# Cross-attention on one core: row sums on TensorE, late query spreads, and keys in twelve tiles of 121

## The reference

```python
Q = relu(queries @ Wq + bq); K = relu(keys @ Wk + bk); V = relu(values @ Wv + bv)
scores = einsum('hbqd,hbkd->hbqk', Qh, Kh) * scale
key_mask = sign(abs(sum(keys, axis=-1)))        # rows that sum to 0 are masked
scores = where(key_mask == 0, NEG, scores)
attn = softmax(scores, axis=-1)
q_mask = sign(abs(sum(queries, axis=-1)))       # and so are query rows that sum to 0
attn = attn * q_mask
out = einsum('hbqk,hbkd->hbqd', attn, Vh) + queries
```

## Time and profile before

| | us |
|---|---|
| median of three runs | 380.84 (379.0 to 381.56) |
| the profiled execution | 380.48 |
| its span, first to last instruction | 378.7 |
| TensorE matmuls busy | 357.3 (94%) |
| ScalarE busy | 303.9 (80%) |
| VectorE busy | 240.4 (63%) |
| mean granted clock | 0.995 |

### The profile page before, as it was taken

The page is one execution under the profiler, slowest core; times in us unless marked ns, Lnnn a source line. Parts: engine busy times, 40 slices in busy tenths (PEclk is TensorE's granted clock), DMA queues, the critical chain, the costliest instruction groups (busy, mean ns, idle before and its releaser), DMA issues.

```text
span 378.7 us, 16915 instructions
## 1 busy us (share of the span) xinstructions
PE 357.3 (94%) x6712; PEld 252.0 (67%) x6712; DVE 240.4 (63%) x785; ACT 303.9 (80%) x405; POOL 5.7 (2%) x20
## 2 busy tenths in 40 slices
PE   7997898799999999999999999999999999799991
PEld 5655666467676767676776767676776767577660
DVE  5797948267593939576684939485775937475202
ACT  2487477678888888888888888888888888689990
POOL 4010000000000000000000000000000000000000
PEclk9999999999999999999999999999999999999997
DMA  7529904956383745646373846547363837245100
GB/s 222 137 76 326 340 7 88 335 190 209 109 286 86 271 130 185 212 153 191 134 243 85 303 99 221 178 159 227 126 210 103 295 89 263 62 151 175 13 3 8
DMA packets 42852, 63.42 MB, mean 167 GB/s; under 512 B 28426, under 2 KB 32842, under 8 KB 42826
## 3 DMA queue, kind: packets, MB, share of 16 engines
q1 hardware_dynamic: 42106, 62.15, 51.8%
q10 hardware_dynamic: 720, 0.89, 0.7%
HBM read 14.55 MB, written 0.82 MB: 41 GB/s over the span
## 4 chain that ended last, share of the span: by engine, by line
PE 82%; DVE 6%; SPq 3%; DMA 3%; issue 2%; ACT 1%; DVEq 0%; ACTq 0%
PE psum L564 31%; PE psum L549 26%; PE psum L516 12%; PE psum L508 11%; SPq L334 3%; DMA k_parts<-k_low 3%; PE psum L636 1%; DVE v_biased L810 1%; PE psum L647 1%; DVE values L820 1%; DVE selectors L989 1%; ACT probs L477 1%; ACT k_parts L467 1%; DVE q_sum L946 1%; SPq L301 1%
## 5 line engine op out<-in xcount | busy, mean ns | idle before, releaser
L477 ACT ACTIVATE probs<-psum 128x800 f32<-128x800 f32 x384 | 293.5, 840 | 53.3 <-PE psum L549 53.3
L564 PE MATMUL psum<-probs,values 128*32 128x200 f32 x3072 | 153.7, 333 | 0.0
L549 PEld LDWEIGHTS psum<-query_bd,k_parts 64*128 64x128 f32 x1536 | 96.1, 187 | 44.9 <-issue 40.0
L564 PEld LDWEIGHTS psum<-probs,values 128*32 128x32 f32 x3072 | 97.8, 110 | 40.8 <-issue 19.1
L549 PE MATMUL psum<-query_bd,k_parts 64*128 64x200 f32 x1536 | 120.0, 286 | 1.6 <-DMA k_parts<-k_low 1.4
L773 DVE TENSOR_SCALAR_CACHE_REDUCE k_raw<-psum,bk_sb 128x361 f32<-128x361 f32 (+2 forms) x63 | 37.7, 600 | 88.3 <-PE psum L508 88.2
L508 PE MATMUL psum<-keyT,wk_mixed 128*32 128x361 f32 (+2 forms) x504 | 52.4, 491 | 6.2 <-DMA keyT<-in_ctxT 2.2
L516 PE MATMUL psum<-wv_sb,keyT 128*32 128x129 f32 x1536 | 55.1, 277 | 3.3 <-DVE v_biased L810 3.3
L820 DVE TENSOR_SCALAR values<-v_biased,keep 128x128 f32<-128x128 f32 x192 | 43.8, 289 | 6.4
L516 PEld LDWEIGHTS psum<-wv_sb,keyT 128*32 128x32 f32 x1536 | 38.4, 109 | 10.8 <-DVE v_biased L810 4.0
L810 DVE TENSOR_TENSOR v_biased<-psum,bv_sb 128x384 f32<-128x384 f32 x64 | 35.1, 548 | 0.0
(11 more groups left out here) (64 smaller groups left out, 81.7 us busy)
## 6 DMA issues: line engine op xcount, KB each, us to landing
k_parts<-k_high SPq DMA_DIRECT2D x30, 722.0 KB, 5.0
k_parts<-k_low SPq DMA_DIRECT2D x30, 722.0 KB, 5.5
keyT<-in_ctxT SPq DMA_DIRECT2D x15, 722.0 KB, 4.4
query_rep<-k_parts SPq DMA_DIRECT2D x4, 800.0 KB, 8.0
residual<-in_x SPq DMA_DIRECT2D x64, 12.5 KB
out<-residual SPq DMA_DIRECT2D x64, 12.5 KB
x_sb<-in_x SPq DMA_DIRECT2D x1, 800.0 KB
values<-in_xT ACTq DMA_DIRECT2D x1, 600.0 KB, 6.7
```

The costliest lines, as they stand in the source:

```text
L477: nc.scalar.activation(probs[:, u % PROB_SLOTS], scores_ps[:, u % SCORE_SLOTS, :, 0:QCOLS], ACT.Exp, scale=SCALE).then_inc(probs_ready, 1)
L549: mm = nc.tensor.matmul(scores_ps[:, u % SCORE_SLOTS, j, n * TCOLS:(n + 1) * TCOLS], k_parts[rows, parity, t, kt * P:(kt + 1) * P], query_ ...
L564: mm = nc.tensor.matmul(o_spans[c * VCOLS:(c + 1) * VCOLS, half, :, :, 0:SPAN], values[:, parity, kt, half * HALF_PAIRS + c, :], probs[:, ...
```

## The change

1. **Tiles of 121.** Score matmuls, exponentials, value projections and value products use twelve tiles of 121 keys (12 x 121 = 1452) in place of 128. In a value projection the last column group has 25 keys, not 32.
2. **Row sums on TensorE.** `x_sb`, its load and VectorE's sums are gone. TensorE multiplies the transposed queries with a column of ones, 16 matmuls of one column, as the first side work of batch 0; VectorE compares. A matrix made by GpSimd (`row_pick`) then spreads the mask over the partitions by four matmuls in the last cycle of batch 0, in place of the 16 copies.
3. **Queries in two spreads.** The first group (batches 0 to 3) is split and copied at the start as before. The other three groups (1200 columns) are cast and subtracted in `first_batch` between key reads, and their four copies stand in SyncE's queue behind the spread keys of batch 2. Every batch of the loop waits for `late_replicated` before it spreads queries.
4. **Order.** At the start the weights are mixed before the selectors are made, and the bias of the keys is loaded first. The residuals of batches 0 and 1 are loaded earlier. In `first_batch` a value read stands between the two centerings, and the queries are spread before the last value read. The query maximum, the bounds (now one operation) and the head sums move to the end of batch 14.

```diff
+    KTILE = -(-SK // KT)
+    SKT = KT * KTILE
...
-                    for g in range(SPANS):
-                        at = c * VCOLS
-                        sp.dma_start(row_mask[at:at + SPAN, g, :], q_mask[g * SPAN:(g + 1) * SPAN, :]
-                                     ).then_inc(rows_masked, 16)
...
-            for ready, count, source, slots in ((q_high_ready, 1, q_high, (0, 1)), (q_split, 3, q_low, (2, 3))):
+            sp.wait_ge(pads_zeroed, 4)
+            sp.wait_ge(first_evacuated, KCHUNKS)
+            load_residual(0, 0)
+            load_residual(1, 1)
+
+            for ready, count, source, slots in ((q_relued, 2, q_high, (0, 1)), (q_split, 2, q_low, (2, 3))):
...
             sp.wait_ge(scores_ready, UNITS)
             spread_keys(2, 0)
+            for ready, source, slots in ((late_high_ready, late_high, (0, 1)), (late_split, late_low, (2, 3))):
+                sp.wait_ge(ready, 1)
+                for n in slots:
+                    sp.dma_start(query_rep[n:P:SLOTS, :, QB * SQ:].bitcast(F32),
+                                 source[:].rearrange("p g n -> p (g n)").bitcast(F32)).then_inc(late_replicated, 16)
...
+            def sum_queries(index):
+
+                work(index)
+                for b in range(B):
+                    mm = nc.tensor.matmul(work_ps[0:SQ, b:b + 1], xT_sb[:, b * SQ:(b + 1) * SQ], ones[:, 0:1],
+                                          start=True, stop=True)
+                mm.then_inc(work_filled, 1)
+
+            def pick_rows(index):
+
+                work(index)
+                pe.wait_ge(rows_picked, 2)
+                for g in range(SPANS):
+                    mm = nc.tensor.matmul(work_ps[:, g * B:(g + 1) * B], row_pick[:, g, :], q_mask[:],
+                                          start=True, stop=True)
...
-                                              k_parts[rows, parity, t, kt * P:(kt + 1) * P],
+                        mm = nc.tensor.matmul(scores_ps[0:KTILE, u % SCORE_SLOTS, j, n * TCOLS:(n + 1) * TCOLS],
+                                              k_parts[rows, parity, t, kt * KTILE:(kt + 1) * KTILE],
                                               query_bd[rows, parity, t, :], start=True, stop=True)
...
-            FIRST_SIDE_WORK = (((0, NEXT),), ((1, NEXT), (2, NEXT)), ((3, NEXT), VALUES[0]), VALUES[1:2], VALUES[2:3],
-                               (VALUES[3], KEYS[0]), KEYS[1:3], KEYS[3:4])
+            FIRST_SIDE_WORK = (((SUM, NEXT), (0, NEXT)), ((1, NEXT), (2, NEXT)), ((3, NEXT), VALUES[0]), VALUES[1:2],
+                               VALUES[2:3], (VALUES[3], KEYS[0]), KEYS[1:3], (KEYS[3], (ROWS, NEXT)))
...
             def first_batch():
-                read_keys(1, 0, 0)
-                max_queries()
...
+                mask_queries(0)
...
+                read_keys(2, 0, used)
+                high_queries()
+                read_keys(2, 1, used + 1)
+                read_keys(2, 2, used + 2)
+                low_late_queries()
+                read_keys(2, 3, used + 3)
...
+                dve.wait_ge(late_replicated, 16 * SLOTS)
                 spread_queries(b + 1, 1 - parity)
                 finish_keep(b + 1, 1 - parity)
-                bound_scores(b + 1, 1 - parity)
```

More of the change, by code:

```diff
@@ L512, in project_values @@
             def project_values(bank, parity, g, n):
-                at = (g * VGROUP + n) * P
-                for m in range(0, P, VCOLS):
-                    mm = nc.tensor.matmul(bank[m:m + VCOLS, n * VW:(n + 1) * VW],
-                                          keyT[:, parity, at + m:at + m + VCOLS], wv_sb[:], start=True, stop=True)
+                at = (g * VGROUP + n) * KTILE
+                for m in range(0, KTILE, VCOLS):
+                    end = min(m + VCOLS, KTILE)
+                    mm = nc.tensor.matmul(bank[m:end, n * VW:(n + 1) * VW],
+                                          keyT[:, parity, at + m:at + end], wv_sb[:], start=True, stop=True)
                 return mm
@@ L573, in _ @@
             NEXT, AFTER = 1, 2
+            SUM, ROWS = -1, -2
             KEYS = tuple((c, AFTER) for c in range(KPARTS))
@@ L600, in batch @@
                     units = range(cycle * CYCLE, (cycle + 1) * CYCLE)
-                    for step in side[cycle][:-1]:
+                    early = 0 if first and cycle == 0 else max(len(side[cycle]) - 1, 0)
+                    for step in side[cycle][:early]:
                         side_work(step)
@@ L607, in batch @@
                         pe.wait_ge(first_k_spread, KCHUNKS * QUADS)
-                    for step in side[cycle][-1:]:
+                    for step in side[cycle][early:]:
                         side_work(step)
```

240 lines of the change are left out of this document (121 added, 119 removed).

## The result

| | before | changed |
|---|---|---|
| median of the runs made together | 380.63 us | 385.72 us (383.98 to 388.19) |
| ratio | | 1.016, 95% interval 1.011 to 1.021 |
| profiled execution, time and span | 380.48, 378.7 us | 386.32, 384.6 us |
| mean granted clock | 0.995 | 0.971 |

The changed kernel is slower by 5.1 us in the medians and by 5.8 us between the two profiled executions. The forecast was 384.8 us.

What follows compares the result with a forecast made beforehand. TensorE was taken to bound steady batches, ScalarE's exponentials the last twelve cycles, waits the first two batches. 380.5 - 3.3 + 1.9 + 3.2 + 2.2 + 0.3 = 384.8 us, range 379 to 390.

Steps and rivals of the forecast that it cites:

- A: The forecast itself: 384.8 us in total, own range 382.5 to 388, chance 0.48.
- 1. Tiles of 121: -3.3: Score matmuls, batches 2 to 13 and half of 14: shorter key loads save 0.033 us in each of 100 cycles, -3.3 us.
- D: Rival at the score loads: 111 ns is a floor whatever the columns, so tiles give nothing; 388.8 us, chance 0.15.
- E: Rival at the score loads: 121 columns lose a quick form of load that 128 have; 592 us, chance 0.02.
- 2 and 3. Batch 0: +1.9: Batch 0: row sums and row picker add 4.4 us on TensorE, fewer waits and faster scores take off 2.3 and 0.3.
- 4. The late copies: 8.3 us of wait, +3.2: Batch 1: old waits go, but TensorE waits 8.3 us through VectorE for late query copies; 29.1 against 25.9 us.
- 5. The clock: +2.2: Behind batch 1's wait for late copies: TensorE's clock falls to the lower level, costing 2.2 us.
- 6. The start: +0.3: Ahead of batch 0: query weights load later behind bias and first x slice, between -0.4 and +0.7, taken as +0.3 us.
- 7. VectorE's stand: 0: Behind VectorE's loop: its 3.21 us stand without a releaser, of which TensorE lost 2.1, stays as it was.
- Rival F: The wait at VectorE's stand moves with the code, -2.1 us (382.7), or another appears, +2; chance 0.04.

Runs made afterwards that it cites:

- tiles128: The changed kernel with key tiles of 128 columns again, all else of the change kept; 391.39 us, 1.030 of the kernel before.
- before121: The kernel before with only its key tiles changed, twelve of 121 in place of 128; 375.65 us, ratio 0.988.
- late_first: The changed kernel with the four late query copies issued ahead of the spread keys of batch 2; 374.77 us, 0.985 of the kernel before.
- peel: The changed kernel with VectorE's batch 1 written out ahead of its loop, without the wait for late copies there; 372.10 us, 0.977 of the kernel before.
- peel_wait: The changed kernel with VectorE's batch 1 written out ahead of its loop, its wait for late copies kept; 382.69 us, 1.007 of the kernel before.
- before121_peel: The kernel before with tiles of 121 and VectorE's batch 1 written out before its loop, row sums still on VectorE; 374.42 us, ratio 0.985.
- one_sum: The changed kernel with one matmul of ones replacing the row-sum matmuls, so every query row counts as kept; 380.42 us, 1.003 of the kernel before.
- both_start: The changed kernel with late copies first, batch 1 written out without the wait, 32-column row sums, and ScalarE's old load order; 368.14 us, 0.969 of the kernel before.
- wide_sums: The changed kernel with each row-sum matmul moving 32 columns of ones instead of one; 386.69 us, 1.016 of the kernel before.

## Why the prediction was right, and what it left out

The forecast, A, held: 384.8 us against 385.72, with the wait where and how it was put. By its own steps, measured between the two profiled executions:

**1. Tiles of 121: -3.3.** Measured -3.20 over 92 cycles, 0.035 us each instead of 0.033. tiles128 and before121 confirm it from both sides. Rivals D, a floor of 111 ns, and E, a slow load at 121 columns, are out: a load of 121 columns takes 182 ns, and the 100-column loads of the sums go every 89 ns, the interval the forecast had worked out. The rule "Always tile to 128 partitions" (the Trainium skill, Trainium Kernel Development and Optimization, Best Practices), by which this step would have been nothing or worse, is contradicted by both kernels: with the number of tiles the same, the narrower load wins.

**2 and 3. Batch 0: +1.9.** Measured +1.91, but by two errors that cancel, which is luck. The block cost what it was to cost. Not foreseen was the fall of the clock behind it, 1.4 us. In return the waits left came to 1.6 us by the forecast's own count (30.19 less 20.79, 2.0, 4.4 and 1.4) where I had 2.9. The rows show 0.78 of it, at a key projection that waits for VectorE's value read, and 0.12 at the row picker; the rest is in no wait that they show.

**4. The late copies: 8.3 us of wait, +3.2.** The wait was 9.09. The copies landed 20.95 us after the batch began instead of 20.1, and TensorE got its bank at 23.0 instead of 22.2. The wait lies just inside the upper bound, 9.1. late_first shows that it comes of the queue's order, peel against peel_wait what it costs. Of batch 1's +6.43, 4.0 is this.

**5. The clock: +2.2.** Behind the wait, 77.29 to 86.62 took 9.33 us where the same work takes 6.91 in a steady batch: 2.4. The granted clock was 0.50 from 72.3 to 82.5 us, in and behind TensorE's wait of 9.09 us. The Trainium skill ("TensorE: Matmul & The Clock Gate", on HAM oscillation) says that a wait for a DMA between bursts of matmuls sends the clock to half rate; here TensorE waits for the DMA by way of VectorE, and the trace agrees. But the step counted one fall and there were three, at 1.4 us each for the other two.

**6. The start: +0.3.** In the profiles it was -1.0, which says nothing of the change: the clock came up at 4.01 us instead of 9.61, and this varies from one execution of a kernel to another. Among profiles whose clock rose between 4.0 and 5.7 us, those with the old order of loads begin batch 0 at 23.15, 23.39 and 23.39, and the eight with the new one at 24.0 to 24.9, mean 24.4. The change costs 1.1 there. The direction was right and the size too small: I had bounded it by the query weights. They landed 3.0 us later (5.83 instead of 2.88), but the first projection began where it had before (6.17 against 6.16); it was bq, landed at 8.50 instead of 6.51, that held ScalarE up.

**7. VectorE's stand: 0.** This step failed. TensorE's loss in batch 13 went from 2.2 to 4.3 us (23.26 - 21.07 and 25.08 - 20.79), +2.1: 0.6 by the wait, 1.4 by the clock. Only the wait belongs to the change for certain: late_first has the stand too, its clock stayed up, and it lost 2.8 us there (23.58). The last cycles, a little shorter, gave 0.4 back, which makes the +1.69 of the table. Rival F had it as a mishap in either direction with a chance of 0.04. The stand hangs on where the code leaves the loop, and the change moved instructions across that place; that was to be seen, and deserved a chance of its own.

The two sides of the total are then: foreseen and true -3.2 and -0.4 for the tiles, +4.0, +2.4 and batch 0's +1.9; unforeseen +2.1 for the stand with its clock; and -1.0 of start that is no part of the change: 5.8. Set against the forecast's terms, +2.1 for the stand, +0.8 and +0.2 for the wait and its clock, -0.3 for the tiles and -1.3 for the start leave 1.5 us between its sum and the profiled execution. That the total came this close is in part luck; the place and size of the large wait are not.

What stays open: why the clock falls behind the sums in eight of the ten profiles that have them and not in the other two, one of them of the same kernel as a profile with the fall. In the four profiles without the sums (before, before121, before121_peel, one_sum) it did not fall in batch 0; neither their width nor their being in one block decides it. In the two profiles without the fall the last of the sums began at 26.85 us, earlier than in any other (both_start), or the clock had risen only at 10.27 (wide_sums). A late rise is not enough: in late_first it came at 9.68, and the clock fell at 30.16.

## What to carry to other kernels

When work is moved into a queue, ask of each wait behind it which iteration really needs it: here a wait for data of batches 4 to 15 was put into the loop body, where batch 1 met it first, and it turned a gain of 1.5 to 2.3% (late_first, peel) into a loss of 1.6%. Where the load of the stationary operand sets the pace, divide the columns evenly over the tiles that are needed anyway. A stall of a loaded TensorE can cost more than its length, since the clock may fall behind it (1.4 us behind some waits of 2 to 3 us, nothing behind others, 2.4 behind 9.09); and one profile of a clock effect is no evidence until the same kernel has been profiled again.

## What was not expected of the hardware

- The granted clock fell to 0.50 while TensorE was hardly idle: 2.8 us of loads of 100 columns with matmuls of 1 or 32 columns, then the fall between 27.9 and 30.2 us, for 3.4 to 10.2 us; each fall of 3.4 us cost 1.4.
- Two profiles of one kernel differ by 3.0 us in batch 0 (28.80 and 31.83) by this alone.
- The clock comes up at the start anywhere from 4.0 to 10.3 us. In the two profiles of one kernel it came at 10.27 and 4.27, and the first full cycle at 25.53 and 24.88.
- VectorE stands 3.2 to 3.7 us behind its loop's end, at a place that depends on the code; with the end one batch later it isn't there at all.
